# A fused attention and feed-forward block on one core: the second long chunk's softmax denominator summed from its first step, and one layer-norm application moved six slots later

## Chip, cores and metric

One core of a Trainium2 chip runs the whole kernel in one launch. The metric is the device time of that launch in microseconds (us). The kernel before took 827.0 us (median of three runs, 826.18 to 828.85).

## What is computed

For each of 8 sequences of 1024 rows and 256 columns, 8 heads of 32:

```python
paths = sigmoid(x @ Wp + bp)                      # (head, row, depth 5)
agree = pq * pk + (1 - pq) * (1 - pk)
sim = cumprod(agree, -1).sum(-1) / 5              # causal mask, then softmax
x = layernorm(x + (softmax(sim) @ (x @ Wv)) @ Wo)
h = silu(x @ wg.T) * (x @ wu.T)                   # 768 hidden, int weights / 127
x = layernorm(x + h @ wd.T)
```

## The kernel before

**Work and slots.** A sequence ("batch" b, 0 to 7) is worked off in 24 steps. `CHUNKS` are four: chunk q = 0 and 1 are the first 512 query rows (c = 0) for head groups g = 0 and 1, with four key tiles j each; q = 2 and 3, the long chunks, are the last 512 query rows (c = 1) with eight key tiles each. So steps 0 to 3, 4 to 7, 8 to 15 and 16 to 23 belong to q = 0, 1, 2, 3. A step i of batch b has three parts on three engines: `scores` (TensorE, line 915, into the two PSUM tiles `slot`), `exps` (ScalarE, line 531, `slot` to one of three buffers of `probs`), and for the last four key tiles of a chunk `mask` (GpSimd, line 460). Two steps later (`LAG = 2`) comes `weigh`: four matmuls of the probabilities with V into `ctx_ps` (line 938), and, where the step is not summed, four matmuls with a block of ones into `den_ps` (line 944), which give the softmax denominator.

**Summed steps.** For steps in `ADDED`, VectorE adds the probability tiles in `acc` instead: the first two by one instruction (line 635), each later one by one more (line 638). After the last one TensorE multiplies `acc` with ones once (line 950). Before the change `ADD_FROM = {2: 2, 3: 1}`: chunk 2 sums from key tile 2, chunk 3 from key tile 1, and the steps ahead of that (8, 9 and 16) use line 944. For the last batch's chunk 3 the masked steps 20 to 23 are not summed either. `exps` of step s+3 writes the `probs` buffer of step s, and waits for `weigh` and for the sum that reads it.

**The order.** A list `PLAN` is written out once and every engine walks it, taking its own entries. Slot s holds: scores, exps and mask of step s; the sum of step s-1; the entries of the table `BETWEEN` for that slot (projections, feed-forward, norms of this and the previous batch); weigh of step s-2; and after a chunk's last step `normalise` (VectorE, lines 646 to 654). In slots 17 to 22 stand the first-half feed-forward pairs `gate_pair(0, n)`, n = 0 to 5. A pair is four gate matmuls and four up matmuls on TensorE (line 975), a tanh on ScalarE (line 552), and on VectorE line 736, which reads and frees the gate's PSUM buffer, and line 744, which frees the up's. There are two such buffers (`misc`) until the ending, handed out in turn, so that gate n+1 waits for line 736 of pair n, and up n+1 for line 744 of pair n. `halves(0, n)` then makes two half-precision parts of the product (ScalarE line 558, GpSimd line 474, the latter called `hid_lo`). In slot 23 stand two sets of transposes (`turn_f`, TensorE line 898) that need the same two buffers, and VectorE frees them by line 615.

**The last norm.** `norm(1, -1, 1)` in slot 16 takes the statistics of the previous batch's second output half; `("apply", 1, -1, 1)` in slot 18 (VectorE, line 718, four instructions) applies them, and `("store", -1, 1)` (line 405, SyncE's DMA queue) stores them. The rows of `x1` that it works on are next written in slot 3 of the following batch, after a wait for the store. SyncE walks the plan in order too: `phi_store` (line 367) in slot 23, and `stack` (line 381, eight loads, which feed the scores of step 4) in slot 0.

`LAST_BETWEEN` replaces slots 17 to 23 for the last batch: pair 0 in slot 17, the apply and the store in slot 18, pair 1 in slot 19, nothing in 21 to 23; `ending()` holds the rest.

## Time and profile before

| | |
|---|---|
| median of 3 runs | 827.0 us |
| the profiled execution | 826.07 us, of which the span of the profile is 824.3 us |
| mean granted TensorE clock | 0.988 |
| TensorE matmul busy | 780.9 us, 95% |
| TensorE weight load busy | 380.5 us, 46% |
| VectorE busy | 611.3 us, 74% |
| ScalarE, GpSimd busy | 468.8 us, 57%; 292.4 us, 35% |
| granted clock below full | 712.6 to 719.4 us: 0.50; 64 to 88 us: 0.86 on average |

A busy share is of the whole span and says nothing of one stretch. Batches 1 to 6 repeat closely: the stretches 206 to 302 us and 590 to 686 us have TensorE busy for 94.78 and 94.76 us of their 96. All places below are given for one of them, the batch whose slot 0 begins at 301.46 us; its slot 18 begins at 376.68 us.

### The profile page before, as it was taken

Reading aid. Unit: us, or ns where it says so; the run is one execution under the profiler, and the core shown is the slowest. Engines: PE = TensorE matmul, PEld = TensorE weight load, DVE = VectorE, ACT = ScalarE, POOL = GpSimd, SP = SyncE. Lnnn points to the kernel's source line nnn. Section 1 sums busy time; section 2 is a strip of 40 time slices with the busy share of each in tenths; the row PEclk is TensorE's granted clock in tenths of the full one; section 3 lists DMA queues with packets and bytes.
Section 4 is the critical chain, followed back from the end, with each engine's and each line's share of the span. In section 5 each row is a group of like instructions: output and inputs, shape, how many; then the busy total and the mean of one; then the engine's idle time right before and its main releaser. Section 6 shows DMA issues by size and latency. Waiting matters only on the chain.

```text
span 824.3 us, 14147 instructions
## 1 busy us (share of the span) xinstructions
PE 780.9 (95%) x5378; PEld 380.5 (46%) x5378; DVE 611.3 (74%) x1057; ACT 468.8 (57%) x737; POOL 292.4 (35%) x266
## 2 busy tenths in 40 slices
PE   6996999999999999999999999999999999799986
PEld 5552355443644445353554436444453535244353
DVE  2768776699568977689766995689766897459677
ACT  1655654667466665566546674666656565365622
POOL 0102251346225262252513462242622535135324
PEclk9999899999999999999999999999999999899999
DMA  6932546034730727116450347306270165301011
GB/s 223 209 121 78 128 115 168 2 91 89 181 100 2 157 78 168 59 24 156 119 163 1 88 94 175 107 1 149 82 178 3 26 154 126 105 1 27 27 26 54
DMA packets 81302, 79.40 MB, mean 96 GB/s; under 512 B 37712, under 2 KB 60496, under 8 KB 81232
## 3 DMA queue, kind: packets, MB, share of 16 engines
q1 hardware_dynamic: 81232, 78.46, 38.0%
q8 instruction: 45, 0.74, 0.4%
q14 instruction: 25, 0.20, 0.1%
HBM read 53.28 MB, written 16.78 MB: 85 GB/s over the span
## 4 chain that ended last, share of the span: by engine, by line
PE 61%; DVE 22%; issue 8%; ACT 5%; DMA 2%; POOL 1%; SPq 0%; DVEq 0%; POOLq 0%; ACTq 0%
PE slot L915 10%; PE misc L975 10%; PE ctx_ps L938 9%; DVE acc L638 8%; PE misc L889 7%; PE misc L988 7%; PE misc L961 6%; PE den_ps L944 6%; DVE work L736 4%; ACT probs L531 4%; DVE x L718 3%; PE den_ps L950 2%; DVE acc L635 1%; DVE work L744 1%; DMA xT_sb<-in_xT_dram 1%
## 5 line engine op out<-in xcount | busy, mean ns | idle before, releaser
L531 ACT ACTIVATE probs<-slot 128x1024 f32<-128x1024 f32 (+3 forms) x384 | 290.3, 810 | 224.1 <-PE slot L915 217.9
L460 POOL TENSOR_SCALAR_AFFINE_SELECT probs<-probs 128x512 f32<-128x512 f32 x128 | 132.5, 1037 | 211.3 <-ACT probs L531 211.2
L915 PE MATMUL slot<-query_stack,key_stack 128*128 128x512 f16 (+3 forms) x768 | 161.3, 330 | 10.2 <-ACT probs L531 9.3
L474 POOL TENSOR_TENSOR work<-work 128x512 f16<-128x512 f32 x96 | 111.9, 1166 | 160.0 <-ACT work L558 160.0
L938 PE MATMUL ctx_ps<-probs,vz_sb 128*32 128x512 f32 (+3 forms) x1536 | 164.7, 501 | 0.3 <-ACT ctx_raw L539 0.3
L975 PE MATMUL misc<-x1T_hi,w_parts 128*128 128x512 f16 x358 | 137.8, 385 | 8.9 <-issue 3.8
L975 PE MATMUL misc<-x1T_lo,w_parts 128*128 128x512 f16 x358 | 137.7, 385 | 0.0
L915 PEld LDWEIGHTS slot<-query_stack,key_stack 128*128 128x128 f16 x768 | 55.9, 98 | 172.1 <-issue 119.7
L638 DVE TENSOR_TENSOR acc<-acc,probs 128x2048 f32<-128x2048 f32 (+3 forms) x68 | 115.8, 1702 | 0.6 <-POOL probs L460 0.5
L736 DVE SCALAR_TENSOR_TENSOR work<-work,misc 128x512 f32<-128x512 f32 x90 | 61.5, 683 | 54.1 <-ACT work L552 52.6
L465 POOL TENSOR_TENSOR rstd<-var_eps,neg_half 128x4 f32<-128x4 f32 x31 | 47.4, 1529 | 143.2 <-DVE var_eps L690 119.7
L988 PE MATMUL misc<-w_parts,work 128*128 128x256 bf16 x696 | 80.8, 273 | 1.4 <-DVE x L672 1.4
L944 PE MATMUL den_ps<-probs,ones 128*32 128x512 f32 (+3 forms) x736 | 74.1, 474 | 0.6 <-DVE den_turned L646 0.6
L988 PEld LDWEIGHTS misc<-w_parts,work 128*128 128x128 f16 x696 | 67.6, 98 | 14.6 <-DVE x L672 4.3
L558 ACT ACTIVATE work<-work 128x512 f16<-128x512 f32 x96 | 61.3, 639 | 22.5 <-DVE work L744 21.7
L889 PE MATMUL misc<-wvp_sb,xT_sb 128*128 128x296 f32 (+1 forms) x256 | 72.8, 423 | 0.4 <-DMA xT_sb<-in_xT_dram 0.4
L744 DVE SCALAR_TENSOR_TENSOR work<-work,hid_scale,misc 128x512 f32<-128x512 f32 x89 | 66.5, 748 | 4.0 <-PE misc L975 0.9
L552 ACT ACTIVATE work<-misc 128x512 f32<-128x512 f32 x90 | 54.5, 606 | 13.5 <-PE misc L975 13.4
L718 DVE TENSOR_SCALAR x<-x,mv,rstd 128x256 f32<-128x256 f32 x124 | 55.3, 507 | 8.9 <-POOL rstd L465 8.9
L938 PEld LDWEIGHTS ctx_ps<-probs,vz_sb 128*32 128x32 f32 x1536 | 30.5, 108 | 66.4 <-issue 62.0
L975 PEld LDWEIGHTS misc<-x1T_hi,w_parts 128*128 128x128 bf16 x358 | 35.2, 98 | 55.5 <-issue 12.7
L961 PE MATMUL misc<-wo_sb,ctxT 128*128 128x256 f32 x248 | 56.6, 381 | 0.4 <-DVE ctxT L654 0.4
(75 smaller groups left out, 704.6 us busy)
## 6 DMA issues: line engine op xcount, KB each, us to landing
key_stack<-phi_dram SPq DMA_DIRECT2D x56, 256.0 KB, 5.5
query_stack<-phi_dram SPq DMA_DIRECT2D x56, 256.0 KB, 6.3
x_sb<-in_x_dram SPq DMA_DIRECT2D x8, 1024.0 KB, 5.7
out_dram<-x SPq DMA_DIRECT2D x15, 512.0 KB, 4.2
xT_sb<-in_xT_dram SPq DMA_DIRECT2D x7, 1024.0 KB, 4.9
phi_dram<-phi_hi SPq DMA_DIRECT2D x14, 256.0 KB, 2.0
phi_dram<-phi_lo SPq DMA_DIRECT2D x14, 256.0 KB, 2.3
key_stack<-phi_dram SPq DMA_DIRECT2D x16, 128.0 KB, 3.1
```

Source lines behind the costliest of these rows:

```text
L460: pool.affine_select(out=tile, in_=tile, compare_op=ALU.is_ge, fill=0.0, base=0, pattern=[[0, 4], [1, P]], channel_multiplier=-1).then_inc ...
L474: pool.tensor_tensor(hid_lo[:, n % M1, :], hid[:, n % HSLOTS, :], hid_hi[:, n % M1, :], ALU.subtract).then_inc(hid_lo_ready, 1)
L531: act.activation(probs[:, s % P_SLOTS, 2 * p:2 * p + 2, off:CH], slot[p][:, :, off:CH], ACT.Exp).then_inc(slot_drained[p], 1)
L638: dve.tensor_tensor(acc[:, :, off:CH], acc[:, :, off:CH], own, ALU.add).then_inc(summed, 1)
L736: dve.scalar_tensor_tensor(out=gated[:, n % 2, :], in0=tanh_g[:, n % 2, :], scalar=1.0, in1=misc[k][:, :], op0=ALU.add, op1=ALU.mult)\
L889: mm = pe.matmul(misc[k][:, 0:cols], xT_sb[:, d, t * P:(t + 1) * P], wvp_sb[:, d, 0:cols], start=(d == 0), stop=(d == KD - 1))
L915: mm = pe.matmul(slot[p][:, k, off:CH], key_stack[:, h, P * j:P * (j + 1)], query_stack[:, h, CH * c + off:CH * (c + 1)], start=True, stop ...
L938: mm = pe.matmul(ctx_ps[32 * k:32 * k + 32, off:CH], vz_sb[:, b % 2, j, 32 * h:32 * h + 32], probs[:, s % P_SLOTS, k, off:CH], start=first ...
L944: mm = pe.matmul(den_ps[32 * k:32 * k + 32, off:CH], ones[:, :], probs[:, s % P_SLOTS, k, off:CH], start=first, stop=final)
L961: mm = pe.matmul(misc[k][:, (t % 2) * D:(t % 2 + 1) * D], ctxT[:, g, t * P:(t + 1) * P], wo_sb[:, g, :], start=(g == 0), stop=(g == NG - 1))
L975: mm = pe.matmul(misc[k][:, :], w_parts[:, w, e, d * F + m * P:d * F + (m + 1) * P], a[:, TC * c:TC * (c + 1), d, :], start=(at == 0), sto ...
L988: mm = pe.matmul(misc[k][:, (t % 2) * D:(t % 2 + 1) * D], a[:, m, t * P:(t + 1) * P], w_parts[:, 2, e, m * D:(m + 1) * D], start=(at == 0 ...
```

## The change

`ADD_FROM` of chunk 3 becomes 0: its first step, 16, is summed too. The four ones-matmuls of step 16 go, the instruction of line 635 reads steps 16 and 17 and runs in slot 18 instead of 19, and step 18 gets an addition of its own in slot 19. The multiplication of `acc` with ones then starts the accumulation in `den_ps` (`start=True`) and waits for `den_out`. The apply and the store move from `BETWEEN[18]` to the end of `BETWEEN[23]`; the last batch keeps them in slot 18. The rest of the diff renames and generalises: `close` is the former tail of `weigh`, `context` the ScalarE part of `normalise`, and `LATE` is empty with these chunks.

```diff
-    ADD_FROM = {2: 2, 3: 1}
+    ADD_FROM = {2: 2, 3: 0}
...
     def added(b, i):
-        return i in ADDED and i <= SUM_END[b, STEPS[i][0]]
-    NA = len(ADD_FROM)
+        q, c, g, j = STEPS[i]
+        return i in ADDED and not (b == 0 and c == 0) and not (b == B - 1 and q == NQ - 1 and i in DIAG)
+    SUM_END = {(b, q): max(i for i in ADDED if STEPS[i][0] == q and added(b, i))
+               for b in range(B) for q in ADD_FROM if any(STEPS[i][0] == q and added(b, i) for i in ADDED)}
+    SUMS = {at: n for n, at in enumerate((b, i) for b in range(B) for i in ADDS if added(b, i))}
+    SUMMED = {at: n for n, at in enumerate(SUM_END)}
...
-        18: [("stack", 1, 0)] + gate_pair(0, 1) + halves(0, 0) + [("apply", 1, -1, 1), ("store", -1, 1)],
+        18: [("stack", 1, 0)] + gate_pair(0, 1) + halves(0, 0),
...
-        23: halves(0, 5) + turn_f(1, 1, 0) + turn_f(1, 1, 1) + [("phi_store", 1, 1)],
+        23: halves(0, 5) + turn_f(1, 1, 0) + turn_f(1, 1, 1) + [("phi_store", 1, 1),
+                                                                       ("apply", 1, -1, 1), ("store", -1, 1)],
...
-                dve.tensor_tensor(acc[:, :, :], probs[:, (s - 1) % P_SLOTS, :, :], own, ALU.add).then_inc(summed, 1)
+                    dve.tensor_tensor(acc[:, :, off:CH], probs[:, (s - 1) % P_SLOTS, :, off:CH], own, ALU.add)\
+                        .then_inc(summed, 1)
...
-                if not added(b, i):
+                end = CH if not added(b, i) else P if c == 0 and first else 0
+                if end:
...
+            def close(b, q):
+                off = P if CHUNKS[q][0] == 0 else 0
+                alone = CHUNKS[q][0] == 1 and ADD_FROM[q] == 0
+                pe.wait_ge(summed, SUMS[b, SUM_END[b, q]] + 1)
+                if alone:
+                    pe.wait_ge(den_out, NQ * b + q)
+                for k in range(4):
+                    mm = pe.matmul(den_ps[32 * k:32 * k + 32, off:CH], ones[:, :], acc[:, k, off:CH],
+                                   start=alone, stop=LAST[q] == SUM_END[b, q])
+                mm.then_inc(acc_used, 1)
```

How VectorE's order moves, in the words of the built programs (line numbers of the change are some 14 higher). `work` holds the feed-forward temporaries and `misc0`, `misc1` are the two buffers. First VectorE before, from the end of slot 17 (batch 3):

```order
L654 TENSOR_TENSOR ctxT<-ctx_raw,den_inv 128x512
L736 SCALAR_TENSOR_TENSOR work<-work,misc1 128x512
L744 SCALAR_TENSOR_TENSOR work<-work,hid_scale,misc0 128x512
L718 TENSOR_SCALAR x1<-x1,mv,rstd 128x256 x4
L635 TENSOR_TENSOR acc<-probs 128x2048
L736 SCALAR_TENSOR_TENSOR work<-work,misc1 128x512
L744 SCALAR_TENSOR_TENSOR work<-work,hid_scale,misc0 128x512
```

and with the change:

```order
L669 TENSOR_TENSOR ctxT<-ctx_raw,den_inv 128x512
L649 TENSOR_TENSOR acc<-probs 128x2048
L751 SCALAR_TENSOR_TENSOR work<-work,misc1 128x512
L759 SCALAR_TENSOR_TENSOR work<-work,hid_scale,misc0 128x512
L653 TENSOR_TENSOR acc<-acc,probs 128x2048
L751 SCALAR_TENSOR_TENSOR work<-work,misc1 128x512
L759 SCALAR_TENSOR_TENSOR work<-work,hid_scale,misc0 128x512
```

An addition now stands ahead of pair 1, and the four applications between pair 1 and the next addition are gone. VectorE in slots 23 and 0, with the change:

```order
L653 TENSOR_TENSOR acc<-acc,probs 128x4x256
L629 SCALAR_TENSOR_TENSOR phi_lo<-misc1,feat_scale,phi_hi 128x512
L629 SCALAR_TENSOR_TENSOR phi_lo<-misc0,feat_scale,phi_hi 128x512
L733 TENSOR_SCALAR x1<-x1,mv,rstd 128x256 x4
L653 TENSOR_TENSOR acc<-acc,probs 128x4x128
L687 SCALAR_TENSOR_TENSOR x1<-misc1,out_scale,x1 128x512
```

The applications now stand between the second `phi_lo` and the chunk's last addition, ahead of the residual of slot 0 (before: the same rows without them). SyncE's queue at the same place, with the change:

```order
L381 DMA phi_dram<-phi_hi 128x1024
L381 DMA phi_dram<-phi_lo 128x1024
L419 DMA out_0_dram<-x1 128x4x256
L395 DMA key_stack<-phi_dram 32x4x1024
```

The store of 512 KB stood ahead of the `phi_hi` store before; now it stands between `phi_lo` and the eight stack loads.

## Rows read from the trace of the kernel before

**Rows 1.** The page, part 1 (busy us, share, instructions) and part 4 (ended-last chain).

```profile
PE 780.9 (95%) x5378; PEld 380.5 (46%) x5378; DVE 611.3 (74%) x1057; ACT 468.8 (57%) x737; POOL 292.4 (35%) x266
PE 61%; DVE 22%; issue 8%; ACT 5%; DMA 2%; POOL 1%; SPq 0%; DVEq 0%; POOLq 0%; ACTq 0%
```

**Rows 2.** Chain that ended last, slots 18 to 0: start us, us, what.

```profile
379.87 0.70 DVE work L736
...
396.12 0.76 DVE work L744
...
397.02 0.63 PE misc L898 x4
```

**Rows 3.** Timeline of TensorE, slots 18 to 22, then slot 4: start us, us, operation, [idle before].

```profile
379.37 1.07 PE L938 MATMUL ctx_ps<-probs,vz_sb 128*32 128x512 f32 x8
380.25 1.04 PE L944 MATMUL den_ps<-probs,ones 128*32 128x512 f32 x8
381.23 1.04 PE L915 MATMUL slot<-query_stack,key_stack 128*128 128x512 f16 x4
...
383.92 1.07 PE L938 MATMUL ctx_ps<-probs,vz_sb 128*32 128x512 f32 x8
384.92 1.04 PE L915 MATMUL slot<-query_stack,key_stack 128*128 128x512 f16 x4
...
392.91 0.39 PE L975 MATMUL misc<-x1T_hi,w_parts 128*128 128x512 f16 x1 [0.21 <-DVE work L736]
...
416.77 0.61 PE L915 MATMUL slot<-query_stack,key_stack 128*128 128x512 f16 x2
```

**Rows 4.** Timeline of VectorE, slots 18 to 0.

```profile
379.12 0.69 DVE L654 TENSOR_TENSOR ctxT<-ctx_raw,den_inv 128x512 f32<-128x512 f32 x1
...
381.25 1.45 DVE L718 TENSOR_SCALAR x<-x,mv,rstd 128x256 f32<-128x256 f32 x4
382.62 2.28 DVE L635 TENSOR_TENSOR acc<-probs 128x2048 f32<-128x2048 f32 x1
384.83 0.67 DVE L736 SCALAR_TENSOR_TENSOR work<-work,misc 128x512 f32<-128x512 f32 x1
...
389.78 2.48 DVE L638 TENSOR_TENSOR acc<-acc,probs 128x2048 f32<-128x2048 f32 x1
...
399.47 0.90 DVE L638 TENSOR_TENSOR acc<-acc,probs 128x512 f32<-128x512 f32 x1
402.06 0.75 DVE L672 SCALAR_TENSOR_TENSOR x<-misc,out_scale,x 128x512 f32<-128x512 f32 x1 [1.69 <-PE misc L988]
```

**Rows 5.** The view of waits: who waited for whom, us in total, times, longest.

```profile
PEld misc L975 <- DVE work L736: 3.2, 7, 0.5
```

**Rows 6.** Timeline of GpSimd, slot 21.

```profile
388.96 1.15 POOL L474 TENSOR_TENSOR work<-work 128x512 f16<-128x512 f32 x1
```

**Rows 7.** Timeline of VectorE, batch 0, slots 18 and 19.

```profile
91.22 0.69 DVE L736 SCALAR_TENSOR_TENSOR work<-work,misc 128x512 f32<-128x512 f32 x1 [0.50 <-ACT work L552]
...
95.75 0.69 DVE L736 SCALAR_TENSOR_TENSOR work<-work,misc 128x512 f32<-128x512 f32 x1 [0.65 <-ACT work L552]
```

**Rows 8.** Timeline of all engines, last batch, slots 18 to 21.

```profile
763.98 0.69 DVE L654 TENSOR_TENSOR ctxT<-ctx_raw,den_inv 128x512 f32<-128x512 f32 x1
764.59 2.22 DVE L718 TENSOR_SCALAR x<-x,mv,rstd 128x256 f32<-128x256 f32 x4
766.73 2.28 DVE L635 TENSOR_TENSOR acc<-probs 128x2048 f32<-128x2048 f32 x1
...
772.65 0.16 PEld L950 LDWEIGHTS den_ps<-acc,ones 128*32 128x32 f32 x8 [0.98 <-DVE acc L638]
```

**Rows 9.** Timeline of SyncE, the last of slot 0's eight stack loads.

```profile
406.61 0.43 SPq L381 DMA_DIRECT2D query_stack<-phi_dram  x1
```

**Rows 10.** The page, part 6: DMA issues, KB each, median us from issue to landing.

```profile
query_stack<-phi_dram SPq DMA_DIRECT2D x56, 256.0 KB, 6.3
```

**Rows 11.** By stretch: busy us (x) of each engine, granted clock, DMA share, GB/s.

```profile
712.60:719.40 6.80, 5.21 (x16) 1.42 (x20) 2.04 (x3) 0.60 (x1) 1.10 (x1) 0.50 0.16 29
```

More of the change, by code:

```diff
@@ L46, in seq_postln_kernel @@
     DIAG = [i for i, (q, c, g, j) in enumerate(STEPS) if j >= TC * c]
-    ADD_FROM = {2: 2, 3: 1}
+    ADD_FROM = {2: 2, 3: 0}
     ADDED = [i for i, (q, c, g, j) in enumerate(STEPS) if q in ADD_FROM and j >= ADD_FROM[q]]
     ADDS = [i for i in ADDED if STEPS[i][3] > ADD_FROM[STEPS[i][0]]]
-    SUM_END = {(b, q): max(i for i in ADDED if STEPS[i][0] == q and not (b == B - 1 and q == NQ - 1 and i in DIAG))
-               for b in range(B) for q in ADD_FROM}
     def added(b, i):
-        return i in ADDED and i <= SUM_END[b, STEPS[i][0]]
-    NA = len(ADD_FROM)
+        q, c, g, j = STEPS[i]
[4 more added lines that the diff above has]
+    SUMMED = {at: n for n, at in enumerate(SUM_END)}
+    LATE = [(b, q) for b, q in SUM_END if CHUNKS[q][0] == 0]
     LAST = {q: max(i for i, s in enumerate(STEPS) if s[0] == q) for q in range(NQ)}
@@ L144, in between @@
             n[at] += b
+            if what == "sum" and tuple(n) not in SUMS or what in ("close", "normalise") and tuple(n) not in LATE:
+                continue
             if 0 <= n[at] < B and (what not in ("load_x", "load_xT", "stack") or n[at] > 0):
@@ L180, in attention @@
                 plan += [("mask", b, i)]
-        if s >= 1 and (s - 1) % NS in ADDS and added(*divmod(s - 1, NS)):
-            plan += [("sum", *divmod(s - 1, NS))]
-        plan += between(b, i)
+        sums = [("sum", *divmod(s - 1, NS))] if s >= 1 and divmod(s - 1, NS) in SUMS else []
+        plan += between(b, i) if STEPS[(s - 1) % NS][1] == 0 else sums + between(b, i)
         if LAG <= s < B * NS - 1:
             b, i = divmod(s - LAG, NS)
-            plan += [("weigh", b, i)] + [("normalise", b, q) for q in range(NQ) if LAST[q] == i]
+            plan += [("weigh", b, i)]
+            for q in range(NQ):
+                if (b, q) in SUM_END and SUM_END[b, q] == i and (b, q) not in LATE:
+                    plan += [("close", b, q)]
+                if LAST[q] == i:
+                    plan += [("context", b, q)] + ([("normalise", b, q)] if (b, q) not in LATE else [])
         return plan
@@ L568, in _ @@
                     exps(*n)
-                elif what == "normalise":
+                elif what == "context":
                     context_out(*n)
@@ L624, in add_up @@
                 own = probs[:, s % P_SLOTS, :, off:CH]
-                count = len(ADDS) * b + ADDS.index(i)
+                count = SUMS[b, i]
                 if i in DIAG:
@@ L643, in normalise @@
                 dve.wait_ge(pv_done, NS * b + LAST[q] + 1)
-                if q in ADD_FROM:
-                    dve.wait_ge(acc_used, NA * b + list(ADD_FROM).index(q) + 1)
+                if (b, q) in SUMMED:
+                    dve.wait_ge(acc_used, SUMMED[b, q] + 1)
                 dve.transpose(den_turned[:, :, :].rearrange("p a n -> p (a n)"), den_ps[:, :]).then_inc(den_out, 1)
@@ L943, in weigh @@
                     for k in range(4):
-                        mm = pe.matmul(den_ps[32 * k:32 * k + 32, off:CH], ones[:, :],
-                                       probs[:, s % P_SLOTS, k, off:CH], start=first, stop=final)
+                        mm = pe.matmul(den_ps[32 * k:32 * k + 32, off:end], ones[:, :],
+                                       probs[:, s % P_SLOTS, k, off:end], start=first, stop=final)
                 mm.then_inc(pv_done, 1)
-                if added(b, i) and i == SUM_END[b, q]:
-                    pe.wait_ge(summed, len(ADDS) * b + ADDS.index(i) + 1)
-                    for k in range(4):
-                        mm = pe.matmul(den_ps[32 * k:32 * k + 32, :], ones[:, :], acc[:, k, :], start=False, stop=final)
-                    mm.then_inc(acc_used, 1)
+            def close(b, q):
[8 more added lines that the diff above has]
+                mm.then_inc(acc_used, 1)
             def project(b, c, s):
@@ L1008, in walk @@
                         weigh(*n)
+                    elif what == "close":
+                        close(*n)
                     elif what == "project":
```

9 lines of the change are left out of this document (4 added, 5 removed).

## The prediction

> **What bounds the kernel now.** I read the page first. TensorE is busy for 95% of the span and VectorE for 74% [rows 1], which looks like a kernel in which any matmul taken away is time gained. The chain that ended last already says something else: 22% of it is VectorE [rows 1]. So the second view is that chain in the slots that the change touches. Between 379.87 us, in slot 18, and 396.88 us, in slot 23, the chain holds no matmul at all [rows 2]: it runs through VectorE's pairs and additions, and TensorE comes back into it only at 397.02, with the transposes that wait for a buffer which line 744 frees. The third view is VectorE's timeline over the same stretch [rows 4]: from 379.12 to 399.47 its rows stand back to back, with no idle time shown. The fourth is TensorE's [rows 3]: its rows stand close as well, but in slot 22 the gate at 392.91 waited for line 736, and the view of waits has such waits 7 times, 3.2 us in total, at most 0.5 us each [rows 5], as one in each of the 7 batches that have pairs there would give. So in slots 18 to 23 the two engines go at nearly the same pace, VectorE is just the later one, and by slot 23 it sets the time.
>
> **What goes from TensorE.** Step 16's four ones-matmuls, once in each of 8 batches. With them, weigh of step 16 to the next scores is 379.37 to 381.23, 1.86 us; without such matmuls, in slot 20, it is 383.92 to 384.92, 1.00 us [rows 3]. That is 0.86 us per batch, 6.9 us in all, if TensorE had nothing else to wait for. The ones-matmuls on `acc` stay as they are, and their new wait for `den_out` ends with the transpose of chunk 2, long before.
>
> **What comes to VectorE, batches 1 to 6.** One more addition of 2048 columns: 382.62 to 384.83, 2.21 us from start to start [rows 4]. The four applications leave slot 18: 381.25 to 382.62, 1.37 us [rows 4]. So up to the next addition VectorE has 2.21 - 1.37 = 0.84 us more to do. The new addition stands ahead of pair 1. Its operands (steps 16 and 17) are there, so it can start as soon as line 654 lets the next instruction in. In the last batch that took 763.98 to 764.59, 0.61 us [rows 8]; here it gives 379.12 + 0.61 = 379.73, against 379.87 at which pair 1 starts now [rows 2], since pair 1 had to wait for its tanh and the addition does not. That returns 0.14 us. VectorE's row of 382.62 comes at 379.73 + 2.21 + 1.38 = 383.32, 0.70 us late. (The bounds of this term are 0.70 and 0.84; I take 0.70, as line 654 is the same instruction in both places.)
>
> What follows on TensorE: weigh of step 16 ends 0.86 us sooner, the scores of slot 19 start at 380.37, and then gate 2 must wait for line 736 of pair 1, which now ends at 379.73 + 2.21 + 0.69 = 382.63. TensorE gets a new idle time of over 1 us right where its work was taken away. From there every addition and pair on VectorE stands 0.70 us later, back to back as before, and so does 397.02 [rows 2], where TensorE depends on line 744. Nothing in the rest of the batch gives this back: the work of slots 0 to 17 follows TensorE's start and moves with it. So **each of six batches becomes 0.70 us longer: 4.2 us**. ScalarE's `exps` of slot 19 now waits for the new addition, until 379.73 + 2.28 = 382.01; it is ready at about 381.0 and ends by 384.0, well ahead of VectorE's need of its tanh at 385.5, so this costs nothing.
>
> **The moved applications and their store.** They come back on VectorE behind `phi_lo`, ahead of the last addition. There VectorE idles 1.69 us ahead of the residual at 402.06 [rows 4], waiting for `down` on TensorE, and 1.37 us fit: the residual is not late by them. The margin is 0.3 us; without that cover the price is at most 1.4 us a batch. Nobody reads these rows of `x1` before slot 3. On SyncE the store passes from before `phi_store` of slot 23 to behind it, ahead of eight stack loads. Those wait for the `phi_dram` stores to land anyway, and the one issue fits in. What the store can cost is bandwidth: the last load is issued at 406.61 [rows 9] and takes 6.3 us at the median [rows 10], so it lands near 412.9, and the scores of slot 4 want it at 416.77 [rows 3]. About 3.9 us are free. The store's 512 KB are the size of two loads of 256 KB, and eight of those are through by 412.9, so it can push the last one by a quarter of the time from the first issue to there, some 2.5 us at most: no cost, but with little to spare.
>
> **Batch 0** has no application to lose, so VectorE gets the full 2.21 us, but it had idle time waiting for tanh there, 0.50 us and 0.65 us [rows 7]. That leaves 1.06 us at most, less what the additions there lose in other company (below, 0.2 us each for two): I take 0.6 us.
>
> **Last batch.** Its applications stay in slot 18, and its pair 1 stands in slot 19, so the new addition goes ahead of everything: +2.21 us on VectorE's row of 766.73 and on the addition after it. TensorE waited 0.98 us for that one at 772.65 [rows 8], so here VectorE is on the path with nothing to pay it back: **+2.2 us**.
>
> **A rule against the trace.** The addition that begins at 389.78 takes 2.48 us, the same form at 382.62 takes 2.28 us [rows 4]. The GpSimd instruction that began at 388.96 and ended at 390.11 lies across the start of the slow one [rows 6], and none lies across the other's. So such a meeting costs 0.2 us. By my schedule the new addition starts with GpSimd idle and makes `hid_lo` of pair 0 wait for its end, near 382.0; that one then takes 1.15 us and is gone by 383.2, just before the next addition at 383.32. So no new meeting, with 0.1 us to spare. The Trainium skill, GPSIMD Engine Reference, section Specifications, says that GpSimd shares its SBUF interfaces with VectorE and that an instruction with two SBUF inputs contends. By that rule each further two-input addition is also a stretch in which GpSimd stands still. The trace agrees with it as far as those rows go.
>
> **Sum.** 4.2 + 0.6 + 2.2 = 7.0 us on the profiled execution's 826.07 us (its span is 824.3 us, and it lies 0.9 us under the median of 827.0): **833.0 us**, slower.
>
> **Rivals.**
>
> - *TensorE is the bound and the matmuls pay.* For it: 95% busy, and TensorE waits for line 736 only 3.2 us in all. Against it: VectorE has no idle time between 379.12 and 399.47, so there is nowhere to put 0.84 us. It decides if VectorE's late instructions still come before TensorE's need, that is with more than 0.84 + 0.86 us of margin; slot 22 shows a margin below zero. Its time: 826.07 - 6.9 = 819.2 us, and if only part arrives, 820 to 824. Chance 8%. The Trainium skill, Perfetto Trace Analysis, section Identifying the Most-Contended Engine, says that matmul busy time is no good measure and that the weight loads' share should be read; that share is 46%, below VectorE's 74% [rows 1], and it speaks for my side.
> - *It cancels.* The delay in VectorE is absorbed in part, for instance since additions meet GpSimd less often (three of the additions in slots 21 to 23 could lose 0.2 us each, 0.6 us a batch). Then only the last batch's 2.2 us stay, less what TensorE gains: 826 to 829 us. Chance 9%.
> - *Dearer than that.* The additions meet `hid_lo` once or twice more in a batch (7 times 0.2 to 0.4, 1.4 to 2.8 us), or the residual of slot 0 comes late, or the stack is late for slot 4 by some 0.5 us in six batches (3 us): 835 to 839 us. Chance 17%.
> - *The clock.* In the last batch, behind two waits of TensorE of over 2 us, the granted clock is 0.50, the 1.2 GHz level, for 6.8 us [rows 11]. The new idle time could bring that into more batches, at up to 3.4 us for each such stretch, 20 us in all. Against it: it is over 1 us, but well below 2 us, and its surroundings are dense. Chance 2%, 850 us.
> - The forecast, 830 to 835 us: 64%.
>
> **Range and chances.** The range reaches from 828.8 us, half way into the cancelling case, to 837.0 us, the middle of the dearer one. The ends of my own terms (0.70 or 0.84 for six batches, 0.4 or 1.1 for batch 0, 1.4 or 2.4 for the last one) give 831.9 to 834.6. A measurement of this kernel can tell about 0.3%, 2.5 us, from no change. Slower by more than that, over 829.5: 64 + 17 + 2 = 83%. Within it: 9%. Faster by more: 8%.
>
> **What would show it.** In the changed kernel: TensorE idle for more than 1 us ahead of gate 2 in slot 19, released by line 736 of the pair, in each batch; slots 18 to 23 of batches 1 to 6 together 0.7 us longer, with slot 18 some 0.86 us shorter and slot 19 some 1.5 us longer; VectorE's idle time ahead of slot 0's residual down from 1.69 to about 0.3 us; slots 0 to 17 unchanged; VectorE's busy time up by about 18 us and TensorE's down by about 7. The prediction is wrong if slot 19 does not grow, if a wait for a stack load shows in slot 4, or if VectorE shows idle time between the pairs of slots 19 to 22.

## Result, and the profile after the change

The changed kernel takes **834.2 us** (median of 6 runs, 831.4 to 835.5), the kernel before 826.7 us beside it (6 runs, 826.0 to 828.9). The ratio is **1.0081, interval 1.0067 to 1.0095**: slower, by 7.5 us. The profiled execution took 834.46 us with a span of 832.7 us, 8.4 us over the one of before.

Part 1 of the page after (busy us, share, instructions) and the shares of the chain that ended last, which answer to [rows 1]:

```profile
PE 777.4 (93%) x5314; PEld 377.5 (45%) x5314; DVE 627.3 (75%) x1065; ACT 468.8 (56%) x737; POOL 309.9 (37%) x266
PE 57%; DVE 23%; issue 11%; ACT 5%; DMA 2%; POOL 1%; SPq 0%; DVEq 0%; POOLq 0%; ACTq 0%
```

64 matmuls fewer (the four of each batch stand as eight in the profile), TensorE busy for 3.5 us less, VectorE for 16.0 us more, and the kernel is slower. GpSimd, whose instructions the change does not touch (266 in both), is busy for 17.5 us more; the section at the end comes back to that.

Now the same batch as in [rows 3] and [rows 4], whose slot 18 begins at 377.35 us here. VectorE's timeline after (start us, us, operation, [idle before <- what ended it]):

```profile
379.78 0.69 DVE L669 TENSOR_TENSOR ctxT<-ctx_raw,den_inv 128x512 f32<-128x512 f32 x1
380.39 2.28 DVE L649 TENSOR_TENSOR acc<-probs 128x2048 f32<-128x2048 f32 x1
382.60 0.68 DVE L751 SCALAR_TENSOR_TENSOR work<-work,misc 128x512 f32<-128x512 f32 x1
...
383.97 2.29 DVE L653 TENSOR_TENSOR acc<-acc,probs 128x2048 f32<-128x2048 f32 x1
...
386.18 0.68 DVE L751 SCALAR_TENSOR_TENSOR work<-work,misc 128x512 f32<-128x512 f32 x1
...
391.14 2.48 DVE L653 TENSOR_TENSOR acc<-acc,probs 128x2048 f32<-128x2048 f32 x1
...
399.51 1.41 DVE L629 SCALAR_TENSOR_TENSOR phi_lo<-misc,feat_scale,phi_hi 128x512 f16<-128x512 f32 x2
400.83 1.46 DVE L733 TENSOR_SCALAR x<-x,mv,rstd 128x256 f32<-128x256 f32 x4
402.21 0.68 DVE L653 TENSOR_TENSOR acc<-acc,probs 128x512 f32<-128x512 f32 x1
403.42 0.75 DVE L687 SCALAR_TENSOR_TENSOR x<-misc,out_scale,x 128x512 f32<-128x512 f32 x1 [0.53 <-PE misc L1012]
```

The new addition begins 0.61 us after line 669 (line 654 before) and pushes everything behind it; no row between 379.78 and 402.21 has idle time ahead of it. The applications stand at 400.83, and VectorE still waits 0.53 us for TensorE before the residual. TensorE's timeline of the same stretch:

```profile
380.04 1.06 PE L953 MATMUL ctx_ps<-probs,vz_sb 128*32 128x512 f32 x8
381.04 1.04 PE L930 MATMUL slot<-query_stack,key_stack 128*128 128x512 f16 x4
383.33 0.39 PE L999 MATMUL misc<-x1T_hi,w_parts 128*128 128x512 f16 x1 [1.26 <-DVE work L751]
...
394.27 0.39 PE L999 MATMUL misc<-x1T_hi,w_parts 128*128 128x512 f16 x1 [0.33 <-DVE work L751]
...
398.38 0.63 PE L913 MATMUL misc<-ident,feat 128*128 128x128 f32 x4 [0.16 <-DVE work L759]
```

The ones-matmuls are gone, the scores follow weigh directly, and then TensorE stands for 1.26 us ahead of gate 2. The view of waits (us in total, times, longest) has that pattern for the whole kernel; [rows 5] had 3.2 us in 7 waits where the first line now stands:

```profile
PEld misc L999 <- DVE work L751: 18.9, 28, 1.8
ACT probs L545 <- DVE acc L649: 14.1, 8, 2.2
PE misc L999 <- DVE work L751: 10.7, 14, 1.3
PEld den_ps L973 <- DVE acc L653: 3.0, 1, 3.0
```

Measured from one start of scores to the next, with the same six slots in each batch (batches 1 to 6 agree to 0.02 us in slots 18 to 23; one batch in each profile has a slot 6 some 1 us longer, before and after alike):

| slot | 18 | 19 | 20 | 21 | 22 | 23 | sum |
|---|---|---|---|---|---|---|---|
| before | 4.55 | 3.69 | 3.69 | 3.48 | 3.65 | 2.62 | 21.68 |
| after | 3.69 | 5.12 | 3.69 | 3.48 | 3.77 | 2.62 | 22.37 |

Batch 0 grew by 0.48 us in these slots (21.44 to 21.92), and slots 18 to 22 of the last batch 3.54 us (14.51 to 18.05). 6 x 0.70 + 0.48 + 3.54 = 8.2 us, which is the 8.4 us between the two profiled executions within 0.2 us. The rest of the two executions is not equal piece by piece: slot 0 of batch 0 begins 0.5 us later, slots 0 to 17 are 0.8 us shorter in batch 0 and 0.7 us longer in the others together, and the ending is 0.2 us shorter. These cancel, and no edit explains them.

### The profile page after: what moved, and what is told of

It reads as the page before. It is cut to its first block, busy times and chain, and to the rows that moved or that the text cites. A ratio compares the mean times of both kernels' runs of the same rounds, so it can differ in the third digit from the quotient of the medians.

```text
span 832.7 us, 14043 instructions
## 1 busy us (share of the span) xinstructions
PE 777.4 (93%) x5314; PEld 377.5 (45%) x5314; DVE 627.3 (75%) x1065; ACT 468.8 (56%) x737; POOL 309.9 (37%) x266
## 4 chain that ended last, share of the span: by engine, by line
PE 57%; DVE 23%; issue 11%; ACT 5%; DMA 2%; POOL 1%; SPq 0%; DVEq 0%; POOLq 0%; ACTq 0%
PE slot L930 10%; PE ctx_ps L953 9%; DVE acc L653 9%; PE misc L999 9%; PE misc L904 7%; PE misc L1012 7%; PE misc L985 6%; PE den_ps L961 6%; DVE work L751 4%; ACT probs L545 3%; DVE x L733 2%; DVE work L759 1%; PE slot L999 1%; PE den_ps L973 1%; ACT work L566 1%
## 5 line engine op out<-in xcount | busy, mean ns | idle before, releaser
L474 POOL TENSOR_SCALAR_AFFINE_SELECT probs<-probs 128x512 f32<-128x512 f32 x128 | 134.8, 1056 | 211.4 <-ACT probs L545 211.2
L488 POOL TENSOR_TENSOR work<-work 128x512 f16<-128x512 f32 x96 | 127.1, 1324 | 151.3 <-ACT work L572 151.3
L653 DVE TENSOR_TENSOR acc<-acc,probs 128x2048 f32<-128x2048 f32 (+1 forms) x76 | 132.6, 1744 | 0.6 <-POOL probs L474 0.5
L999 PEld LDWEIGHTS misc<-x1T_hi,w_parts 128*128 128x128 bf16 x358 | 35.2, 98 | 71.0 <-DVE work L751 18.9
L961 PE MATMUL den_ps<-probs,ones 128*32 128x512 f32 (+3 forms) x672 | 66.2, 465 | 0.6 <-DVE den_turned L661 0.6
```

The lines of the kernel that those rows point to most:

```text
L474: pool.affine_select(out=tile, in_=tile, compare_op=ALU.is_ge, fill=0.0, base=0, pattern=[[0, 4], [1, P]], channel_multiplier=-1).then_inc ...
L488: pool.tensor_tensor(hid_lo[:, n % M1, :], hid[:, n % HSLOTS, :], hid_hi[:, n % M1, :], ALU.subtract).then_inc(hid_lo_ready, 1)
L653: dve.tensor_tensor(acc[:, :, off:CH], acc[:, :, off:CH], own, ALU.add).then_inc(summed, 1)
L961: mm = pe.matmul(den_ps[32 * k:32 * k + 32, off:end], ones[:, :], probs[:, s % P_SLOTS, k, off:end], start=first, stop=final)
L999: mm = pe.matmul(misc[k][:, :], w_parts[:, w, e, d * F + m * P:d * F + (m + 1) * P], a[:, TC * c:TC * (c + 1), d, :], start=(at == 0), sto ...
```

## Experiments

The theory: from slot 18 to slot 23 VectorE sets the pace, with TensorE close behind, so what counts is VectorE's work there; matmuls taken away turn into waits. Its rivals: the ones-matmuls matter as such, the place of the new addition is what costs, or the price lies in the last batch. Three things can be set apart: the ones-matmuls of step 16, the new addition, and the place of the applications. Each median stands beside runs of the kernel before on the same chip (826.4 to 826.8 us).

### One part at a time

**No ones-matmuls of step 16, nothing in their place, applications in slot 18.** Step 16 is missing from the denominator of chunk 3.

```diff
-    ADD_FROM = {2: 2, 3: 0}
+    ADD_FROM = {2: 2, 3: 1}
...
-                if end:
+                if end and i != 16:
...
-                alone = CHUNKS[q][0] == 1 and ADD_FROM[q] == 0
+                alone = q == 3
```

(and the apply and the store back in slot 18)

> The kernel before, without the four ones-matmuls of step 16 and without an addition in their place; the applications stay in slot 18. Step 16 is missing from chunk 3's denominator, so this kernel leaves a part of the computation out. Theory (VectorE sets the time from pair 1's tanh in slot 18 to the transposes of slot 23): nothing that VectorE does there starts earlier, so slot 18 gets 0.86 us shorter, slot 19 waits for line 736 of pair 1 or a later slot waits for a later pair, and slots 18 to 23 together stay within 0.1 us in batches 1 to 6: 0 to 1.5 us less in all, 824.5 to 826.5 us. Rival (TensorE is the bound, the matmuls are worth their time): 0.86 us less in each of 8 batches, 6.9 us, 819.8 us.

Measured: 825.3 us, ratio 0.999 (0.998 to 1.000). TensorE's timeline in slots 20 and 22 of this kernel:

```profile
381.84 0.39 PE L998 MATMUL misc<-x1T_hi,w_parts 128*128 128x512 f16 x1 [0.45 <-DVE work L750]
...
389.20 0.39 PE L998 MATMUL misc<-x1T_hi,w_parts 128*128 128x512 f16 x1 [0.34 <-DVE work L750]
```

Slots 18 to 23 sum to 21.69 us against 21.68: slot 18 is 0.86 us shorter, and slots 20 to 22 give back 0.64 + 0.10 + 0.13. Taking 6.9 us of matmuls from a TensorE that is "95% busy" brings about a microsecond in all, and none of it in these slots of batches 1 to 6. Batch 0 shows the other side: it has no applications, VectorE waits for tanh there [rows 7], and its slots 18 to 23 do get shorter by the whole 0.86 us (20.58 against 21.44). In the last batch they are not shorter (14.51 both times). So "TensorE is the bound" holds in batch 0 and is ruled out in the others, more directly than by the change itself.

**The applications and the store moved, nothing else.**

```diff
-    ADD_FROM = {2: 2, 3: 0}
+    ADD_FROM = {2: 2, 3: 1}
```

> The change without its new addition (ADD_FROM of chunk 3 stays 1): only the applications and their store move from slot 18 to the end of slot 23, in batches 1 to 6. Theory: VectorE has 1.37 us less ahead of slot 19's addition, falls back onto its waits for tanh, and TensorE goes at its own pace in slots 19 to 23: slot 22 3.3 us in place of 3.65, slot 23 2.5 in place of 2.62, together 0.5 us a batch and 3 us in all: 823.6 us. Rival (TensorE is the bound anyway, the 0.2 us waits are noise): no change, 826.6 us. Rival (the store beside the stack loads or the later applications cost something): slots 0 or 4 grow, 828 us or more.

Measured: 825.0 us, ratio 0.9982 (0.9973 to 0.9992). The batch is 0.22 us shorter, about half of what was expected. VectorE's timeline, slots 18 to 21, says why:

```profile
379.54 0.69 DVE L751 SCALAR_TENSOR_TENSOR work<-work,misc 128x512 f32<-128x512 f32 x1
...
380.92 2.48 DVE L649 TENSOR_TENSOR acc<-probs 128x2048 f32<-128x2048 f32 x1
384.07 0.69 DVE L751 SCALAR_TENSOR_TENSOR work<-work,misc 128x512 f32<-128x512 f32 x1 [0.66 <-ACT work L566]
...
385.46 2.47 DVE L653 TENSOR_TENSOR acc<-acc,probs 128x2048 f32<-128x2048 f32 x1
387.85 0.68 DVE L751 SCALAR_TENSOR_TENSOR work<-work,misc 128x512 f32<-128x512 f32 x1
...
389.23 2.48 DVE L653 TENSOR_TENSOR acc<-acc,probs 128x2048 f32<-128x2048 f32 x1
```

VectorE saved 1.37 us of applications, then had to wait 0.66 us for a tanh, whose gate matmuls stand behind the ones-matmuls of step 16: for that moment TensorE is the late one. From pair 1 to pair 2 it is 4.53 us in place of the 4.96 between 379.87 [rows 2] and 384.83 [rows 4], so 0.43 us are gained up to there. By coming sooner two more additions also met a `hid_lo` on GpSimd and took 2.48 and 2.47 us in place of 2.28. The first of them is hidden by the wait for the tanh; the second isn't, its pair follows after 2.39 us in place of 2.20, and 0.24 us are left.

**Both together: no ones-matmuls, no addition, applications moved.** The same `if end and i != 16` and `alone = q == 3` with `ADD_FROM = {2: 2, 3: 1}`; step 16 is missing from the denominator again.

> The kernel before, without the ones-matmuls of step 16, without an addition in their place, and with the applications and their store at the end of slot 23: both engines are relieved at once. Step 16 is missing from chunk 3's denominator, so a part of the computation is left out. Alone, the one gave nothing in slots 18 to 23 of a batch (96.0 us a batch as before) and the other 0.2 us. Theory (two engines at nearly one pace, the later one sets the time): together they give more than their sum, up to TensorE's own pace, slots 19 to 23 at 3.69, 3.69, 3.48, 3.27 and 2.1 to 2.4 us: 1.0 to 1.5 us a batch, 816 to 820 us. Rival (the effects add): 0.2 us a batch, 824 us.

Measured: 819.0 us, ratio 0.9908 (0.9891 to 0.9924); slots 18 to 23 sum to 20.60. Alone the two were worth nothing and 0.22 us a batch, together they are worth 1.08 us. Two engines go at the same pace, so each edit by itself only turns into a wait on the other one.

**The new addition without the move.**

```diff
-        18: [("stack", 1, 0)] + gate_pair(0, 1) + halves(0, 0),
+        18: [("stack", 1, 0)] + gate_pair(0, 1) + halves(0, 0) + [("apply", 1, -1, 1), ("store", -1, 1)],
...
-                                                                       ("apply", 1, -1, 1), ("store", -1, 1)],
```

> The change with the applications and the store put back into slot 18: only the new addition, and the four matmuls of step 16 gone. Theory: VectorE has 2.21 us more and starts 0.14 us sooner, so slots 18 to 23 get 2.07 us longer in batches 1 to 6 (12.4 us), 0.5 us in batch 0 and 2.2 to 3.5 us in the last: 841.5 to 843 us. Rival (TensorE is the bound for part of it): each microsecond on VectorE counts less than whole, 834 to 838 us.

Measured: 840.7 us, ratio 1.0183 (1.0164 to 1.0203). TensorE's timeline, slots 19 and 20:

```profile
384.97 0.39 PE L998 MATMUL misc<-x1T_hi,w_parts 128*128 128x512 f16 x1 [1.26 <-DVE work L750]
...
389.85 0.39 PE L998 MATMUL misc<-x1T_hi,w_parts 128*128 128x512 f16 x1 [1.01 <-DVE work L750]
```

The first wait is the one of the changed kernel, the second is the applications'. The slots sum to 23.67, 1.30 us over the changed kernel: the move saves nearly the whole of the 1.37 us that the prediction gave it, once VectorE is clearly the later engine.

**Half of the new addition.** It takes 256 of the 512 columns of each head, so steps 16 and 17 are missing from one half of the denominator's columns.

```diff
-                    dve.tensor_tensor(acc[:, :, off:CH], probs[:, (s - 1) % P_SLOTS, :, off:CH], own, ALU.add)\
+                    hi = CH // 2 if q == 3 else CH
+                    dve.tensor_tensor(acc[:, :, off:hi], probs[:, (s - 1) % P_SLOTS, :, off:hi],
+                                      probs[:, s % P_SLOTS, :, off:hi], ALU.add)\
```

> The change, with its new addition taken over the first 256 of 512 columns only, so that half of steps 16 and 17 is left out of chunk 3's denominator. The addition of 1024 columns takes 1.14 us from start to start in place of 2.21. Theory (what counts is VectorE's total between pair 1's place and slot 23): 1.14 - 1.37 - 0.14 = 0.4 us less than before in batches 1 to 6, of which meetings with GpSimd give back some; the last batch costs 1.1 us in place of 2.2 to 3.5: slots 18 to 23 0 to 0.4 us shorter than before a batch, 824.5 to 827 us, and still none of the matmuls' 6.9 us. Rival (a fixed cost of the order or of the new waits, not the length of the addition): little less than the change, 831 to 834 us.

Measured: 821.9 us, ratio 0.9945 (0.9928 to 0.9961), under the expected total; per batch it did what was expected, -0.36 us (sum of slots 21.31). The addition took 1.13 us from start to start in place of 2.21, that is 1.08 less, and the slots are 1.06 us shorter than in the changed kernel. Behind the point at which VectorE is late its work counts in full.

The kernels on one scale, batches 1 to 6:

| ones of step 16 | new addition | applications | slots 18 to 23, us | median, us |
|---|---|---|---|---|
| yes | none | slot 18 (before) | 21.68 | 826.7 |
| yes | none | slot 23 | 21.46 | 825.0 |
| no | none | slot 18 | 21.69 | 825.3 |
| no | none | slot 23 | 20.60 | 819.0 |
| no | half | slot 23 | 21.31 | 821.9 |
| no | whole | slot 23 (the change) | 22.37 | 834.2 |
| no | whole | slot 18 | 23.67 | 840.7 |

The fourth and the sixth row price the addition: 1.77 us a batch. That is 2.21 us, less the 0.14 us by which it starts closer behind line 669 than pair 1 does, less about 0.3 us because the additions behind it then take 2.29, 2.28 and 2.48 us where the fourth kernel has 2.48, 2.38 and 2.48.

### The place of the addition

**The addition behind pair 1** in place of ahead of it, so that gate 2 finds its buffer free early.

```diff
-        plan += between(b, i) if STEPS[(s - 1) % NS][1] == 0 else sums + between(b, i)
+        if (s - 1) % NS == 17 and ("hidden", b, 1) in between(b, i):
+            found = between(b, i)
+            at = found.index(("hidden", b, 1)) + 1
+            plan += found[:at] + sums + found[at:]
+        else:
+            plan += between(b, i) if STEPS[(s - 1) % NS][1] == 0 else sums + between(b, i)
```

> The change with its new addition placed behind pair 1 of slot 18 instead of ahead of it, in batches 0 to 6. Theory: the wait of TensorE ahead of gate 2 in slot 19 (1.26 us) goes, but VectorE has the same work up to pair 2, so the wait comes back one slot later and nothing is won; the exps of slot 19 moreover waits for the addition that now ends 1.4 us later, near 383.5, which puts pair 2's tanh and all behind it some 0.5 us later: 0 to 3.5 us more than the change, 834 to 838 us, slots 18 to 23 0 to 0.5 us longer than in the change. Rival (the change loses its time by the place of the addition, ahead of a pair that TensorE needs): slot 19 falls back to 3.69 us, the gain of 0.86 us a batch arrives, 822 to 828 us.

Measured: 842.1 us, ratio 1.0186 (1.0168 to 1.0204): worse than the changed kernel, and worse than expected. ScalarE's timeline in slot 19 of this kernel (its batch 3; slot 18 begins at 381.92):

```profile
389.05 1.94 ACT L550 ACTIVATE probs<-slot 128x1024 f32<-128x1024 f32 x2 [3.46 <-DVE acc L654]
```

And TensorE's behind it, slot 20:

```profile
390.13 0.61 PE L935 MATMUL slot<-query_stack,key_stack 128*128 128x512 f16 x2 [0.76 <-ACT probs L550]
391.04 0.61 PE L935 MATMUL slot<-query_stack,key_stack 128*128 128x512 f16 x2 [0.31 <-ACT probs L550]
392.25 0.55 PE L1004 MATMUL misc<-x1T_hi,w_parts 128*128 128x512 f16 x1 [0.61 <-DVE work L756]
392.59 0.63 PE L1004 MATMUL misc<-x1T_lo,w_parts 128*128 128x512 f16 x1
```

With three `probs` buffers, `exps` of slot 19 waits for the addition that reads step 16. In the changed kernel that wait is there too (the second line of the waits above, 8 times) and costs nothing, since the addition ends at 382.67. Here it ends near 389, `exps` starts 3.46 us late, and the scores of slot 20 wait for `exps`. The last two rows show something else: the matmuls take 0.63 us where they took 0.38, and by stretch (busy us (x) of each engine, granted clock, DMA share, GB/s) the trace has

```profile
392.40:395.80 3.40, 3.40 (x12) 1.00 (x14) 3.40 (x3) 2.54 (x4) 2.68 (x2) 0.50 0.02 5
```

a granted clock of 0.50, the 1.2 GHz level, behind those three waits of TensorE. That happened in two of the batches, 3 and 4, whose slot 20 takes 6.6 us in place of 4.96 (the same three waits stand in the other five, and their matmuls take 0.38 us); slots 21 to 23 give back most of it, and they sum to 23.66 and 23.68 where the others have 23.35. So the clock costs 0.3 us twice. The rest is 1.67 us in each of batches 1 to 6 over the kernel before, 0.97 over the changed kernel, and 3.5 us in the last batch as in the changed kernel. My expectation had the wait of `exps` in it, but at 0 to 0.5 us a batch. The addition ends 7.05 us after slot 18 begins, 1.73 later than in the changed kernel where 1.4 was written, as it also meets a `hid_lo`. Pair 2 then starts 9.59 us after slot 18 does in place of 8.83, and the addition behind it meets a `hid_lo` too (2.48 us in place of 2.28). These 0.76 and 0.20 us are the 0.97.

### The last batch

**The last batch as before, all others as changed**: in it step 16 uses its ones-matmuls again.

```diff
-        return i in ADDED and not (b == 0 and c == 0) and not (b == B - 1 and q == NQ - 1 and i in DIAG)
+        return i in ADDED and (b, i) != (B - 1, 16) and not (b == 0 and c == 0) and not (b == B - 1 and q == NQ - 1 and i in DIAG)
...
-                alone = CHUNKS[q][0] == 1 and ADD_FROM[q] == 0
+                alone = CHUNKS[q][0] == 1 and ADD_FROM[q] == 0 and (b, q) != (B - 1, NQ - 1)
```

(with the additions' counts to match)

> The change in batches 0 to 6, and the last batch with step 16 by ones-matmuls as before. Theory: the last batch gives back the 2.2 us by which its additions came later and the 1 us or so for which TensorE ran at half clock behind its long wait: 830.5 to 832 us, slots 18 to 23 of the last batch at 2.82, 3.69, 2.12, 3.48 and 2.40 us again. Rival (the last batch's longer time has another cause, as the clock's chance or the ending): 833.5 to 835 us.

Measured: 831.0 us, ratio 1.0057 (1.0041 to 1.0074), and slots 18 to 22 of the last batch are back at 14.49 us. So the last batch alone is worth 3.1 us by the medians (7.54 us over the kernel before with it, 4.46 without), where its delayed addition explains 2.2. The changed kernel's last batch, TensorE's timeline:

```profile
776.76 1.06 PE L953 MATMUL ctx_ps<-probs,vz_sb 128*32 128x512 f32 x8
779.90 1.94 PE L973 MATMUL den_ps<-acc,ones 128*32 128x512 f32 x8 [2.08 <-DVE acc L653]
781.77 1.04 PE L930 MATMUL slot<-query_stack,key_stack 128*128 128x256 f16 x4
```

and by stretch:

```profile
779.50:782.90 3.40, 3.00 (x16) 0.80 (x20) 0.35 (x1) 0.61 (x2) 1.95 (x2) 0.50 0.00 0
```

The ones-matmuls on `acc` start 13.30 us after slot 18 does, where it was 11.11 before: 2.19 us later. But behind this wait (2.98 us for the weight load, the last line of the waits above; 0.98 us before, [rows 8]) the granted clock is 0.50 for 3.4 us, and the same eight matmuls take 1.94 us where at full clock they take 1.06 in the kernel with the last batch as before. The half-sized addition had the same wait of 3.0 us and the same slow eight, 1.93 us; with the divide moved (below) TensorE is not idle ahead of the eight, and they take 1.04.

The clock does not fall each time, though. The kernel with the new addition without the move has the same last batch, and in its profile TensorE stands idle for the same 2.08 us ahead of the same eight matmuls:

```profile
785.77 1.06 PE L972 MATMUL den_ps<-acc,ones 128*32 128x512 f32 x8 [2.08 <-DVE acc L652]
```

and by stretch:

```profile
785.30:788.70 3.40, 2.93 (x28) 0.88 (x28) 0.42 (x1) 1.36 (x3) 2.23 (x3) 1.00 0.00 0
```

The granted clock stays at 1.00, and slots 18 to 22 sum to 16.71 us, 2.20 over the 14.51 of before. So of the 3.54 us in the changed kernel's profile 2.20 are the delay and 1.34 the clock. Of the four profiles with this wait of 3.0 us, three have the slower clock and one has not. In how many of the six runs of the changed kernel (831.4 to 835.5 us) it fell here is not known.

### A version that beats both

If VectorE is the later engine only from slot 18 to 23, work of its own that nobody needs there should leave. Such work is `normalise` of chunk 2, four instructions at the end of slot 17 (lines 646 to 654 before, 377.34 to 379.73 us), whose result is wanted by the projection in the next batch's slots only.

**The divide moved** behind the first residual of the next batch's slot 0; in the last batch, together with the apply and the store, to slot 20.

```diff
+    DIVIDED_LATER = [(b, 2) for b in range(B)]
...
-        0: [("stack", 0, 1)] + down(-1, 0, 0),
+        0: [("stack", 0, 1)] + down(-1, 0, 0) + [("normalise", -1, 2)],
...
-        18: halves(0, 0) + [("apply", 1, -1, 1), ("store", -1, 1)],
+        18: halves(0, 0),
...
-        20: halves(0, 1),
+        20: halves(0, 1) + [("normalise", 0, 2), ("apply", 1, -1, 1), ("store", -1, 1)],
...
-                    plan += [("context", b, q)] + ([("normalise", b, q)] if (b, q) not in LATE else [])
+                    plan += [("context", b, q)] + ([("normalise", b, q)] if (b, q) not in DIVIDED_LATER else [])
```

> The change, and chunk 2's VectorE part of normalise (lines 646 to 654 before, 2.5 us) moved from slot 17 to behind slot 0's first residual of the following batch, where VectorE waits over 3 us for TensorE; in the last batch to slot 20, together with the applications and the store. This is possible since with the change nothing writes den_ps between chunk 2's end and chunk 3's end. Theory: the new addition then fits ahead of pair 1's tanh, VectorE has 1.37 us less behind it than before, and both engines are relieved: slots 18 to 23 1.0 to 1.5 us shorter than before in batches 0 to 6, 1 to 2 us in the last: 815 to 819 us. Rival (the divisions are late for something in slots 0 to 3, or the multiplication of acc waits for them): slot 1 or 2 longer by 0.5 us or more, 820 us or more.

Measured: **816.5 us**, ratio **0.9878 (0.9862 to 0.9895)**. VectorE's timeline, slots 17 to 0:

```profile
372.83 2.28 DVE L651 TENSOR_TENSOR acc<-probs 128x2048 f32<-128x2048 f32 x1
375.36 0.69 DVE L753 SCALAR_TENSOR_TENSOR work<-work,misc 128x512 f32<-128x512 f32 x1 [0.24 <-ACT work L568]
...
396.49 0.75 DVE L689 SCALAR_TENSOR_TENSOR x<-misc,out_scale,x 128x512 f32<-128x512 f32 x1 [0.52 <-PE misc L1014]
397.16 0.71 DVE L663 STREAM_TRANSPOSE den_turned<-den_ps 128x512 f32<-128x512 f32 x1
...
400.44 0.75 DVE L689 SCALAR_TENSOR_TENSOR x<-misc,out_scale,x 128x512 f32<-128x512 f32 x1 [0.81 <-PE misc L1014]
```

The divide sits in slot 0, where VectorE still has 0.81 us to wait for the next residual's matmuls. Pair 1 waits for its tanh again, the slots 18 to 23 sum to 20.63 us, and the waits for the gate's buffer have shrunk to

```profile
PEld misc L1001 <- DVE work L753: 2.0, 7, 0.3
```

where the changed kernel had 18.9 us in 28 of them. Now the matmuls taken away pay: the slots are 1.05 us a batch shorter than before, and 0.83 us shorter than with the applications moved alone (21.46), nearly the 0.86 us of the matmuls. The denominator is complete here: this is the change, made to work.

**The same, with the applications and the store of batches 1 to 6 back in slot 18.**

```diff
-        18: [("stack", 1, 0)] + gate_pair(0, 1) + halves(0, 0),
+        18: [("stack", 1, 0)] + gate_pair(0, 1) + halves(0, 0) + [("apply", 1, -1, 1), ("store", -1, 1)],
```

(and out of slot 23)

> The kernel with the later divisions (e8_divide_later), with the applications and the store of batches 1 to 6 back in slot 18. Theory: the new addition still fits ahead of pair 1's tanh, but behind it VectorE has the same work as in the kernel before, so batches 1 to 6 are back at 96.0 us (slot 18 0.86 us shorter, slots 19 to 23 as much longer); only batch 0, which has no applications, and the last batch keep what e8 gained: 822.5 to 825 us. Rival (the later divisions alone bring the gain): 816 to 818 us.

Measured: 824.4 us, ratio 0.9964 (0.9950 to 0.9978); the slots sum to 21.68, as before the change. With 2.4 us of divide gone, 2.2 us of addition come and the applications back, VectorE's sum is nearly what it was, and so is the time of the slots, although TensorE has 0.86 us less to do.

**The same once more on chunk 2**, whose step 9 is now summed too.

```diff
-    ADD_FROM = {2: 2, 3: 0}
+    ADD_FROM = {2: 1, 3: 0}
```

> The kernel with the later divisions (e8_divide_later), and chunk 2 summed from key tile 1 instead of 2: another addition of 2.2 us in slot 11, where VectorE stands idle for 3.3 us, and four more ones-matmuls (0.86 us) gone from the end of slot 11, in each of 8 batches. Theory: VectorE has hardly any idle time in slots 12 to 16 and its work there starts from the projection of slot 11, which does not move, so slot 11 gets 0.86 us shorter and slots 12 to 16 give it back: 94.9 us a batch as in e8, 815.5 to 817 us. Rival (here TensorE is the bound and the addition is hidden in idle time): 0.86 us less a batch, 809 to 811 us.

Measured: 816.1 us, ratio 0.9866 (0.9850 to 0.9883), the same as without it. Slot 11 is 0.86 us shorter (5.42 against 6.28) and slot 13 is 0.71 us longer (3.07 against 2.36): 0.1 us a batch is left. In slot 13 TensorE now waits 0.19 us for line 753, and 0.43 us for `exps` ahead of the scores that follow; the kernel without step 9 has neither.

## Why the prediction was right, and where it was not

The time (833.0 forecast, 834.2 measured) came out by its own mechanism, and the parts can be held against rows. It is nearer than its parts are, which is luck: on the profiled executions the slots in question grew by 8.2 us where 7.0 was written, and what is missing lies in the last batch, while the medians lie only 7.5 us apart.

- **The 0.86 us of matmuls do not arrive.** Right. Slot 18 is 0.86 us shorter, slot 19 1.43 us longer (some 1.5 was written), with TensorE idle for 1.26 us ahead of gate 2. The kernel without ones-matmuls shows it alone: 21.69 against 21.68 us.
- **Batches 1 to 6, +0.70 us each.** Right to some hundredths (96.00 to 96.70 us), and by its terms: the new addition starts 0.61 us behind line 669, pair 1 is pushed by 2.21 us, and the addition after pair 1 stands at 383.97, where 382.62 + 0.70, moved on by the 0.67 us by which this batch starts later, gives 383.99.
- **`exps` of slot 19 waits at no cost.** Right: ScalarE waits for line 649 in every batch, and no idle time stands ahead of the pair at 386.18. The experiment with the addition behind the pair shows the margin by overrunning it.
- **The moved applications are hidden.** Right. VectorE's idle time ahead of the residual went from 1.69 to 0.53 us; I had 0.3, since I had not seen that the last addition would be 0.68 us long in its new place, not 0.90. No wait for a stack load shows in slot 4.
- **Batch 0, +0.6.** 0.48 us measured, of bounds 0.4 and 1.1. Two of its additions take 2.28 us where they took 2.49 and 2.47, as the term had it.
- **Meetings with GpSimd.** None new in the changed kernel, as forecast: one addition of 2.48 us a batch, before and after. That this hung on 0.1 us is shown by the moved applications alone, with three of them.
- **Last batch, +2.2.** The step that was too small. The delay was 2.19 us, but the section rose by 3.54 (3.1 by the medians). The delay itself was right; the rise lies outside the term's own bounds of 1.4 and 2.4. What failed is that the clock stood in the prediction only as a case for the middle batches at 2%, with "its surroundings are dense"; I had not asked what the 0.98 us wait of the last batch becomes when 2.2 us are added to it. It became a wait of 2.98 us, and in this execution the clock behind it fell to the 1.2 GHz level, which cost 1.34 us.
- **Busy times.** VectorE +16.0 us (18 was written), TensorE -3.5 us (7 was written): matmuls at half clock count nearly twice, and the changed kernel has one such stretch more and a longer one (714.6 to 724.9 us against 712.6 to 719.4 [rows 11]). TensorE's busy time at a granted clock of 0.50 is 17.2 us after and 14.4 before; half of the 2.8 us between them is 1.4 of the 3.5 us that are missing. Where the other 2 us lie is not shown. Of VectorE's missing 2 us, 1.3 are the last addition, 0.22 us shorter in each of six batches, and 0.4 are batch 0's two.
- **A sum.** The lower ends of the terms, 4.2 + 0.4 + 1.4 us, give 832.1 us, not the 831.9 that was written. Nothing hangs on it.

Two sizes of the experiments were missed as well: the move alone brought half of what I expected, and the addition behind pair 1 cost 4 us more than my upper end. In both the meetings with GpSimd were left out, and in the second the wait through the three `probs` buffers was put too low as well. Why the median of the half-sized addition lies 2.6 us under its expected range while its batches did as forecast isn't settled; its profiled execution took 824.9 us, within the range.

The Trainium skill, Perfetto Trace Analysis, section Identifying the Most-Contended Engine, says that matmul busy time is not a good measure and that for VectorE the occupancy is. The trace agrees for the first part: at 95% busy, 6.9 us of matmuls taken away brought 1.1 us. For the second it doesn't help here: VectorE's 74% of the span doesn't tell that it is without idle time for 20 us of each batch.

## What to carry to other kernels

Before work goes from one engine to another, look at both timelines over the very slots in question: where both stand nearly without gaps, relieving one alone is worth little or nothing (0 and 0.22 us here) and relieving both is worth the whole (1.08 us). Look at each kind of batch by itself: in batch 0, where VectorE had waits to spare, the same matmuls paid in full. Work moved to an engine has to be paid for by other work of that engine that leaves the same stretch: here the move of a 2.4 us divide (and in the last batch of the applications with it) turned +0.8% into -1.2%. And where a wait of TensorE is lengthened, ask what it grows to, since the clock behind it may fall as well: 1.34 us on top of 2.20 here, in three of four profiles.

## What the runs showed of the hardware

**An addition of VectorE that reads two tiles from SBUF and an instruction of GpSimd wait for each other.** GpSimd's timeline in the changed kernel, the same `hid_lo` instruction (1.15 us in [rows 6]) and the mask:

```profile
381.09 2.61 POOL L488 TENSOR_TENSOR work<-work 128x512 f16<-128x512 f32 x1 [4.33 <-ACT work L572]
385.78 1.50 POOL L488 TENSOR_TENSOR work<-work 128x512 f16<-128x512 f32 x1 [2.09 <-ACT work L572]
...
392.40 1.71 POOL L474 TENSOR_SCALAR_AFFINE_SELECT probs<-probs 128x512 f32<-128x512 f32 x1 [0.94 <-ACT probs L545]
...
769.85 3.10 POOL L488 TENSOR_TENSOR work<-work 128x512 f16<-128x512 f32 x1 [3.85 <-ACT work L572]
```

The three `hid_lo` began 0.70, 1.81 and 0.21 us into an addition (380.39, 383.97 and 769.64 us) and ended 1.03, 1.02 and 1.03 us after it did (at 382.67, 386.26 and 771.92). The mask that began 1.26 us into the addition of 391.14 ended 0.49 us after it. Whenever they began, nearly all of their own time (1.15 us, and 0.63 us for a mask that meets no addition) was still ahead of them at the addition's end: they wait, rather than run slower. This is where GpSimd's 17.5 us come from: by the page's groups 15.2 us lie in the 96 `hid_lo` (mean 1324 ns after, 1166 before) and 2.3 us in the masks.

The other way round VectorE waits. In the twelve traces 160 additions of 2048 columns began while a `hid_lo` was running, with 0.22 to 0.34 us of it left, and each ended 2.14 to 2.15 us after the `hid_lo` did: 2.48 us long with 0.33 us left, 2.40 with 0.25 left (at 380.52 in the kernel with the divide moved). The 371 that found GpSimd free, or began first, took 2.27 to 2.29 us. The price was small here because little of the `hid_lo` was left; in no trace does an addition begin early in one. The Trainium skill, GPSIMD Engine Reference, section Specifications, says that the two share their SBUF interfaces and contend when VectorE's instruction has two SBUF inputs; the trace agrees, and adds that the one that begins later waits for the other, whichever engine it is on.

**Half clock behind short waits.** In the changed kernel it came behind one wait of 2.98 us (2.08 us of it with TensorE idle), and with the addition behind pair 1 behind waits of 0.76, 0.31 and 0.61 us close together. Neither brings it each time: the same 2.98 us stayed at full clock in one of four profiles, and the same three waits in five of seven batches. A single wait of 1.26 us in each of batches 1 to 6 of the changed kernel brought none. What tells these cases apart no run here shows.
